# Windowed differential attention: all rotated tiles, spreads and v ahead of the loop, the shifted v by a transfer inside SBUF, the normalisation in three pieces

## The chip, the cores and the metric

One Trainium2 chip, one core. The metric is the time of one execution on the device in microseconds, the median over several runs. The kernel is one program for the whole network below.

## What is computed

The input x is 1024 tokens by 256 features. Eight sublayers follow each other, each x = layernorm(x + f(x)): causal attention, an 8-bit gated MLP, windowed differential attention, a mixture of experts, causal attention, a binary-weight linear layer, attention with a multiplied mask, a ternary gated MLP. The change is in the third. Cut to what matters:

```python
q = (x @ Wq).reshape(b, s, 16, 16).transpose(0, 2, 1, 3)     # 16 heads of 16
k = (x @ Wk).reshape(b, s, 4, 16).transpose(0, 2, 1, 3)      # 4 key/value heads
v = (x @ Wv).reshape(b, s, 4, 16).transpose(0, 2, 1, 3)
q = q * cos + rotate_half(q) * sin;  k = k * cos + rotate_half(k) * sin
k, v = repeat(k, 4), repeat(v, 4)
a1 = q[..., :8] @ k[..., :8].T * 8 ** -0.5
a2 = q[..., 8:] @ k[..., 8:].T * 8 ** -0.5
allowed = (col <= row) & (col >= row - 63)
p1, p2 = softmax(a1 + neg), softmax(a2 + neg)
diff = relu(p1 - lam * p2)
diff = diff / (diff.sum(-1) + 1e-6)
out = (diff @ v) @ Wo
x = layernorm(x + out)
```

## The kernel before

Each engine has its own program, written out by hand, and they meet on semaphores. TensorE (PE), VectorE (DVE), ScalarE (ACT) and GpSimd (POOL) compute; SP issues the transfers. PE writes into two double banks of PSUM called pair (a ring: a new use waits until ACT has read the one before the last), three banks called bank (a ring read by DVE) and pvb.

**Tiles.** The tokens are in two halves of 512; the second half comes first, here and in the neighbouring sublayers. A tile of q or k is 128 (q) or 64 (k) rows of features by 512 tokens, so there are three a half: k, q of heads 0 to 7, q of heads 8 to 15. `W_HALVES` lists the six, and ("R", i) stands for the i-th. For each, PE makes two products with the plain and the swapped weights (`tile_rows`, L1654, matmuls at L1481), DVE multiplies them by cos and sin and adds them (`rotate`, L1228 and L1231), ACT rounds to bf16 (`highest`, L915), DVE takes the remainder and rounds it (`middle`, L1239 and L1240), and POOL takes the last remainder (`lowest`, L781). The three bf16 parts sit in `piece`; w_buf, where the rotation is written, has two buffers, and rotation i waits for the low part of i - 2.

**Spreads.** An item ("s", side, g, x, half) lays two heads' parts out over the partitions, with six selector matmuls on PE (L1673) into one pair, and ACT copies the pair to SBUF as bf16 (L930 ahead of the loop, L937 in it). Twenty are needed in all: for each half, two of k and eight of q. Six of them precede the loop today.

**The order.** `windowed_plan` returns two lists. All engines walk through both, each doing its share of every item. `W_BEFORE` is the opening; today R0 (whose half is ready early), then x1 (transposes of the other half of x, L1486, and ACT's copies to xT, L827), R1, R2, and six spreads. `W_PLAN` is the loop over 32 units. A unit k is a tile t of 128 queries by a group g of four heads, in the order of `T_ORDER`: token tiles 5, 6, 7, 4, then 0 to 3. In step k:

- ("S", k): PE writes the mask and the scores of both softmaxes into a pair (L1722, L1728); DVE takes the maxima (L1268); ACT takes eight exponentials with their sums (L948); in the next step DVE makes the ratio of the sums (L1251, L1252) and POOL forms lam * p2 - p1 (L797, L800).
- ("uT", k - 3): PE transposes that (L1752), DVE applies the relu and stores it (L1286).
- every fourth step pv: PE multiplies by v (L1768), ACT copies pvb (L954), and a step later accT: PE transposes back (L1775), DVE divides (L1296 to L1298).
- after the 16 units of the first half: outT (L1486 bank<-A, L1302), four projections with residual and statistics (L1049, L1053), then ("norm"), all of `normalise(s, 0)` in one step: 4 aggregations, 3 small steps and 3 times 3 Newton steps (L1065 to L1075), 4 products (L1077).

Into these steps today's plan puts the rest of the preparation: spreads of q groups 2 and 3 in steps 0 and 1, R3, R4, R5 in steps 2, 4, 6, v in step 3, the ten spreads of the other half in steps 6 to 15 (one each). Spreads in the loop share the ring of pairs with the scores.

**v.** The window of a 64-query block reaches 64 tokens back, so v is needed twice: `v_own` with the tokens of a tile on its 128 partitions, and `v_back`, the same shifted by 64 tokens. Both are projected: PE makes two sets of eight small products in two banks (L1736 to L1745), and DVE copies them (L1281, L1283, L1284).

After the loop `last_half_out` transposes, projects and normalises the other half; the mixture of experts follows.

On SP, in this sublayer, two loads of weights are issued when the sublayer before is normalised (`load(WF...)`, `load(WA[0]...)`); what follows in SP's queue waits for xn_ready of this sublayer.

## Time and profile before

| | us |
|---|---|
| median of 3 runs (lowest, highest) | 1172.81 (1171.85, 1173.26) |
| profiled execution, its own time | 1171.49 |
| its span, first to last instruction | 1169.7 |
| PE busy | 1005.7 (86%) |
| DVE busy | 698.5 (60%) |
| ACT busy | 541.8 (46%) |
| POOL busy | 332.7 (28%) |
| mean granted clock of PE | 0.907 |

The times in all rows count from the span's start. A row of the timeline gives start, duration, engine, line, operation, output<-input, the shapes and a count where equal instructions are merged, then in brackets how long the engine had been idle and who released it. The granted clock of PE is 1.00 (2.4 GHz) or 0.50 (1.2 GHz) at any moment; a figure between is a mean. The changed stage runs from 266.5 (its first tile) to 460.

### The profile page before, as it was taken

What the parts mean: (1) busy time and instruction counts of PE and PEld (TensorE: products, weight loads), DVE (VectorE), ACT (ScalarE), POOL (GpSimd) and SP (SyncE); (2) the same over time, 40 slices, a digit from 0 to 9 for tenths busy, and PEclk for the clock granted to TensorE, in tenths of its full rate; (3) what the DMA queues carried; (4) which work ended last, traced back from release to release, by engine and by line L of the source; (5) the groups of instructions that cost most, each with busy time, mean ns of one, the idle gap of its engine ahead of it and who ended that gap; (6) DMA issues with size and microseconds to landing.
All of it is one profiled execution on the core that took longest, in us unless ns stands there. A gap on an engine that the chain in (4) does not pass through costs nothing. (4 is left out here: it accounts for less than half of the span.)

```text
span 1169.7 us, 16510 instructions
## 1 busy us (share of the span) xinstructions
PE 1005.7 (86%) x5954; PEld 573.3 (49%) x5954; DVE 698.5 (60%) x1986; ACT 541.8 (46%) x1145; POOL 332.7 (28%) x464
## 2 busy tenths in 40 slices
PE   6999998787998868899998899887777988888785
PEld 2545454673444535337356444444454544445575
DVE  2667773775376873532322358778282677876665
ACT  3566655333579862110112456664314455556422
POOL 3202122331367870000002111112461144532222
PEclk9989998998789977899998969999778889999898
DMA  5000000103000002000000002000000000000000
GB/s 229 1 1 1 1 1 1 50 1 159 1 1 2 2 1 92 14 1 1 0 1 1 0 1 109 1 1 1 1 1 1 0 1 1 2 1 1 1 18 19
DMA packets 4165, 21.12 MB, mean 18 GB/s; under 512 B 345, under 2 KB 1625, under 8 KB 3060
## 3 DMA queue, kind: packets, MB, share of 16 engines
q1 hardware_dynamic: 4084, 20.06, 4.4%
q8 instruction: 48, 0.79, 0.3%
q14 instruction: 33, 0.27, 0.1%
HBM read 19.01 MB, written 1.05 MB: 17 GB/s over the span
## 5 line engine op out<-in xcount | busy, mean ns | idle before, releaser
L890 ACT ACTIVATE PB<-pair 128x1024 f32<-128x1024 f32 (+3 forms) x288 | 223.1, 811 | 140.8 <-PE pair L1609 139.6
L1126 DVE CUSTOM_DVE_ANT_0 junk<-bank,cst 128x128 bf16<-128x128 f32 (+3 forms) x384 | 171.5, 487 | 127.8 <-PE bank L1593 125.7
L724 POOL TENSOR_SCALAR_AFFINE_SELECT PB<-PB 128x256 f32<-128x256 f32 x192 | 79.0, 415 | 330.4 <-ACT PB L890 328.7
L1129 DVE TENSOR_REDUCE pmx<-bank 128x1 f32<-128x512 f32 x192 | 122.8, 684 | 49.7 <-PE bank L1593 48.9
L1593 PE MATMUL bank<-KO_r,QO_r 64*128 64x512 f32 (+3 forms) x576 | 138.4, 417 | 11.7 <-DVE A L1204 3.9
L1625 PE MATMUL pvb<-PB,V 128*32 128x512 f32 (+3 forms) x1152 | 128.2, 517 | 11.8 <-ACT PB L890 8.2
L1605 PE MATMUL pair<-QO_r,KO_r 64*128 64x512 f32 (+3 forms) x576 | 115.7, 393 | 15.8 <-ACT PB L890 14.8
L1593 PEld LDWEIGHTS bank<-KO_r,QO_r 64*128 64x128 f32 x576 | 71.6, 191 | 111.7 <-DVE pmx L1126 40.2
L730 POOL TENSOR_TENSOR parts_r<-y_f,parts_r 128x512 fp32r<-128x512 f32 x24 | 30.6, 1276 | 321.2 <-ACT parts_r L861 321.2
L1609 PE MATMUL pair<-ms,sel_r 64*128 64x512 f32 (+3 forms) x576 | 102.5, 349 | 0.0
L948 ACT ACTIVATE KO<-pair,nm 128x128 f32<-128x128 f32 x256 | 91.6, 434 | 22.1 <-DVE nm L1268 22.0
L1605 PEld LDWEIGHTS pair<-QO_r,KO_r 64*128 64x128 f32 x576 | 56.5, 190 | 69.0 <-ACT PB L890 55.6
L1049 DVE TENSOR_TENSOR X<-bank,X 128x256 f32<-128x256 f32 x56 | 23.7, 424 | 86.0 <-PE bank L1870 43.9
L970 ACT ACTIVATE PB<-pair 128x512 f32<-128x512 f32 (+1 forms) x28 | 16.7, 597 | 125.5 <-PE pair L1481 125.5
L1481 PE MATMUL pair<-xT,WA 128*128 128x512 f32 x96 | 59.3, 759 | 10.4 <-DMA WA<-in_w_att 8.0
L797 POOL TENSOR_SCALAR KO<-KO,cc,cst 128x128 f32<-128x128 f32 x128 | 55.9, 454 | 38.6 <-DVE cc L1252 38.1
L948 ACT ACTIVATION_READ_ACCUMULATOR KO<-pair,nm 128x1 f32 x256 | 65.1, 273 | 0.0
L1609 PEld LDWEIGHTS pair<-ms,sel_r 64*128 64x128 f32 x576 | 57.7, 191 | 4.1
L1268 DVE TENSOR_REDUCE nm<-pair 128x4 f32<-128x512 f32 x64 | 42.4, 685 | 24.9 <-PE pair L1728 24.4
L1481 PE MATMUL pair<-xT,WF 128*128 128x512 f32 (+1 forms) x112 | 57.1, 633 | 0.0
L1412 DVE TENSOR_TENSOR PB<-bank,PB 128x512 f32<-128x512 f32 (+1 forms) x28 | 19.4, 691 | 60.5 <-PE bank L1481 60.4
L1481 PE MATMUL bank<-xT,WF 128*128 128x512 f32 (+1 forms) x112 | 54.5, 610 | 0.0
(208 smaller groups left out, 1686.5 us busy)
## 6 DMA issues: line engine op xcount, KB each, us to landing
WF<-in_moe_gu SPq DMA_DIRECT2D x1, 3520.0 KB, 10.8
WA<-in_w_att SPq DMA_DIRECT2D x3, 1024.0 KB, 10.3
WF<-in_tern_w SPq DMA_DIRECT2D x1, 3072.0 KB, 11.1
V<-in_moe_d SPq DMA_DIRECT2D x1, 1792.0 KB, 7.2
xT<-in_xT SPq DMA_DIRECT2D x2, 512.0 KB, 5.9
X<-in_x SPq DMA_DIRECT2D x1, 1024.0 KB, 10.9
A<-in_rope SPq DMA_DIRECT2D x1, 1024.0 KB, 4.7
out<-X SPq DMA_DIRECT2D x2, 512.0 KB, 2.9
```

Source lines behind the costliest of these rows:

```text
L724: pool.affine_select(p2, p2, pattern=[[0, 2], [1, P]], compare_op=ALU.is_ge, fill=0.0, base=0, channel_multiplier=-1).then_inc(causal, 1)
L797: last = pool.tensor_scalar(e2[:, hh, :], e2[:, hh, :], cc[:, k % 4, 1, hh:hh + 1], lam, ALU.mult, ALU.mult)
L890: act.activation(pb[:, st % 2, 2 * i:2 * i + 2, 0:n], ps[:, :, 0:n], ACT.Exp, scale=scale)\
L948: last = act.activation(ew[k % EW][:, z, hh, :], slot[:, z, hh * P:(hh + 1) * P], ACT.Exp, bias=nm2[:, (2 * k + z) % 4, hh:hh + 1], accum_ ...
L1126: r_done(dve.tensor_tensor_reduce(junk[:, (r_used - 1) % 3, 0:n], ps[:, 0:n], tri[:, HALF - n:HALF], 1.0, LOWEST, ALU.add, ALU.max, accum_ ...
L1129: r_done(dve.tensor_reduce(to, ps[:, 0:n], AX.X, ALU.max))
L1268: dve.tensor_reduce(nm2[:, (2 * k + z) % 4, :], pair[(n // 2 - 1) % 2][:, z, :].rearrange("p (h n) -> p h n", h=HG), AX.X, ALU.max, negate ...
L1481: last = pe.matmul(ps, w(c), x(c), start=(c == 0), stop=(c == ND - 1))
L1593: pe.matmul(r_slot()[:, 0:n], qd[rows, TWO * g + i, t * P:(t + 1) * P], kd[rows, TWO * g + i, c * HALF:c * HALF + n], start=True, stop=Tru ...
L1605: pe.matmul(ps[:, j, 0:n], kd[rows, TWO * g + i, kb * P:(kb + 1) * P], qd[rows, TWO * g + i, q0:q0 + n], start=True, stop=False)
L1609: last = pe.matmul(ps[:, j, 0:n], sel_r[rows, 2 * TWO + i, :], ms[rows, b, q0 - qh * HALF:q0 - qh * HALF + n], start=False, stop=True)
L1625: last = pe.matmul(pvb[j * STRIP:(j + 1) * STRIP, q0 - qh * HALF:HALF], v_all[:, kb, g * HG + j, :], pb[:, st % 2, j, 0:n], start=(kb == 0 ...
```

## The change

All six tiles are rotated in `W_BEFORE`, in the order k, k of the other half, q, q of the half that is used first, q, q of the other; so are twelve of the twenty spreads and v. The other eight spreads (q of the other half) come in steps 1, 3, ... 15. `T_ORDER` becomes 4, 5, 6, 7, 0 to 3. On each engine the item's share stands where the item stands, and each of DVE's `middle(i - 1)` follows `rotate(i)`. v is projected once, and v_back is filled by two transfers on SP, from partitions 0 to 63 of v_own to 64 to 127 and the reverse, one tile on; PE waits for them before the first pv. The normalisation of the first half is spread over three steps. The split_x that is removed stood under a condition that doesn't hold for this sublayer. The diff, without its empty lines and the two new semaphores:

```diff
--- before.py
+++ after.py
@@ -131,7 +131,8 @@
 E_EXP = NG * 12 * 2
-E_USES = {ATT: 8 + 4 * NG + TH + E_EXP + 2 * NG + 8, WATT: 12, GLU: 2 * NF + 4, MOE: 2 * NF_MOE + 4, BIN: 4, TERN: 2 * NF + 4}
+W_E = ND + 12 + 2 * ND
+E_USES = {ATT: 8 + 4 * NG + TH + E_EXP + 2 * NG + 8, WATT: W_E, GLU: 2 * NF + 4, MOE: 2 * NF_MOE + 4, BIN: 4, TERN: 2 * NF + 4}
@@ -385,36 +386,28 @@
-W_TILES = (2, 0, 1)
-W_HALVES = [(tile, half) for half in halves_in(SUBLAYERS.index(WATT)) for tile in W_TILES]
-W_LAST, W_FIRST = TH * halves_in(SUBLAYERS.index(WATT))[1], TH * halves_in(SUBLAYERS.index(WATT))[0]
-T_ORDER = [W_FIRST + k for k in (1, 2, 3, 0)] + [W_LAST + k for k in range(TH)]
+W_SOON, W_LATE = halves_in(SUBLAYERS.index(WATT))
+W_OUT, W_END = halves_out(SUBLAYERS.index(WATT))
+W_FIRST = TH * W_OUT
+W_HALVES = [(2, W_SOON), (2, W_LATE)] + [(tile, half) for half in (W_OUT, W_END) for tile in range(2)]
+T_ORDER = [TH * half + k for half in (W_OUT, W_END) for k in range(TH)]
 UNITS = [(t, g) for t in T_ORDER for g in range(NG)]
-    first, second = W_HALVES[0][1], W_HALVES[-1][1]
-    def rows(side, g, half):
-        return [("s", side, g, x, half) for x in range(TWO)]
-    before = [("R", 0), ("x1",), ("R", 1), ("R", 2)] + rows("k", 0, first) + rows("q", 0, first) + rows("q", 1, first)
-    after = {k: [] for k in range(len(UNITS))}
-    after[0] = rows("q", 2, first)
-    after[1] = rows("q", 3, first)
-    for i, k in ((3, 2), (4, 4), (5, 6)):
-        after[k].append(("R", i))
-    after[3].append(("v",))
-    for x in range(TWO):
-        after[6 + x].append(("s", "k", 0, x, second))
-        for g in range(NG):
-            after[8 + TWO * g + x].append(("s", "q", g, x, second))
+    def rows(side, groups, half):
+        return [("s", side, g, x, half) for g in groups for x in range(TWO)]
+    before = [("R", 0), ("x1",), ("R", 1), ("R", 2), ("R", 3)] + rows("k", (0,), W_SOON) + rows("k", (0,), W_LATE) \
+        + rows("q", (0, 1), W_OUT) + [("R", 4)] + rows("q", (2, 3), W_OUT) + [("R", 5), ("v",)]
+    late = rows("q", range(NG), W_END)
     plan = []
             plan.append(("S", k))
-            plan += after[k]
+            if k % 2 and late:
+                plan.append(late.pop(0))
         else:
@@ -425,8 +418,9 @@
         step = j - NG * TH - 2
-        if 0 <= step < 6:
-            plan.append([("outT",), ("proj", 0), ("proj", 1), ("proj", 2), ("proj", 3), ("norm",)][step])
+        if 0 <= step < 8:
+            plan.append([("outT",), ("proj", 0), ("proj", 1), ("proj", 2), ("proj", 3), ("norm", 0), ("norm", 1),
+                         ("norm", 2)][step])
     last = NT - 1
@@ -470,7 +464,7 @@
     for item in W_BEFORE + W_PLAN:
-        n += {"R": 2, "v": 2, "uT": 1, "accT": 1, "outT": ND, "proj": 1}.get(item[0], 0)
+        n += {"R": 2, "v": 1, "uT": 1, "accT": 1, "outT": ND, "proj": 1}.get(item[0], 0)
         if item == ("uT", gi):
@@ -680,6 +675,12 @@
                     load(WA[0][:, :], t_in["w_att2"], ld_att2)
+                    sp.wait_ge(v_there, 1)
+                    sp.wait_ge(w_blank, 1)
+                    v_from, v_to = (v.rearrange("p t h c -> p (t h c)") for v in (v_own, v_back))
+                    row = KV * STRIP
+                    load(v_to[WIN:P, :], v_from[0:WIN, :], v_moved)
+                    load(v_to[0:WIN, row:], v_from[WIN:P, 0:(NT - 1) * row], v_moved)
             for k, half in enumerate(halves_out(len(SUBLAYERS) - 1)):
@@ -781,11 +782,9 @@
-            for i in range(3):
+            for i in range(len(W_HALVES)):
                 lowest(i)
             for item in W_PLAN:
-                if item[0] == "R":
-                    lowest(item[1])
                 if item[0] in ("S", "flush") and 1 <= item[1] <= len(UNITS):
@@ -929,8 +928,6 @@
                 for item in W_PLAN:
-                    if item[0] == "R":
-                        highest(item[1])
                     if item[0] == "s":
@@ -1059,24 +1056,30 @@
-            def normalise(s, k):
+            def normalise(s, k, which=(0, 1, 2)):
                 t0 = halves_out(s)[k] * TH
-                for t in range(t0, t0 + TH):
-                    last = dve.bn_aggr(mv[:, t, :], stats[:, t, :])
-                step(last)
                 v, y, w = lnv[:, 0, :], lnv[:, 1, :], lnv[:, 2, :]
-                step(dve.tensor_scalar(v, mv[:, t0:t0 + TH, 1], EPS, None, ALU.add))
-                step(dve.tensor_scalar(y.bitcast(I32), v.bitcast(I32), 1, None, ALU.logical_shift_right))
-                step(dve.tensor_scalar(y.bitcast(I32), y.bitcast(I32), -1.0, float(0x5F3759DF), ALU.mult, ALU.add))
-                for _ in range(3):
+                def refine():
                     step(dve.scalar_tensor_tensor(w, y, -0.5, y, ALU.mult, ALU.mult))
                     step(dve.scalar_tensor_tensor(y, w, 1.5, y, ALU.add, ALU.mult))
-                for t in range(t0, t0 + TH):
-                    dve.tensor_scalar(X[:, t, :], X[:, t, :], mv[:, t, 0:1], lnv[:, 1, t - t0:t - t0 + 1],
-                                      ALU.subtract, ALU.mult).then_inc(xn_ready, 1)
-                dve.wait_ge(xn_ready, NT * s + TH * (k + 1))
+                if 0 in which:
+                    for t in range(t0, t0 + TH):
+                        last = dve.bn_aggr(mv[:, t, :], stats[:, t, :])
+                    step(last)
+                    step(dve.tensor_scalar(v, mv[:, t0:t0 + TH, 1], EPS, None, ALU.add))
+                    step(dve.tensor_scalar(y.bitcast(I32), v.bitcast(I32), 1, None, ALU.logical_shift_right))
+                    step(dve.tensor_scalar(y.bitcast(I32), y.bitcast(I32), -1.0, float(0x5F3759DF), ALU.mult, ALU.add))
+                if 1 in which:
+                    for _ in range(3):
+                        refine()
+                if 2 in which:
+                    for t in range(t0, t0 + TH):
+                        dve.tensor_scalar(X[:, t, :], X[:, t, :], mv[:, t, 0:1], lnv[:, 1, t - t0:t - t0 + 1],
+                                          ALU.subtract, ALU.mult).then_inc(xn_ready, 1)
+                    dve.wait_ge(xn_ready, NT * s + TH * (k + 1))
@@ -1257,8 +1260,13 @@
                             middle(i - 1)
-                middle(2)
-                turned = []
+                    if item[0] == "v":
+                        middle(len(W_HALVES) - 1)
+                        ps = r_slot()[:, :].rearrange("p (t h d) -> p t h d", t=NT, h=KV)
+                        last = dve.tensor_copy(v_own[:, :, :, 0:HD], ps)
+                        r_done(last)
+                        r_wait()
+                        dve.nop().then_inc(v_there, 1)
                 for item in W_PLAN:
@@ -1268,20 +1276,8 @@
                                               AX.X, ALU.max, negate=True).then_inc(wmax_ready, 1)
-                        if turned:
-                            middle(turned.pop())
                     if item[0] in ("S", "flush") and 1 <= item[1] <= len(UNITS):
                         ratio(item[1] - 1)
-                    if item[0] == "R":
-                        rotate(item[1])
-                        turned.append(item[1])
-                    if item[0] == "v":
-                        dve.wait_ge(w_blank, 1)
-                        ps = r_slot()
-                        r_done(dve.tensor_copy(v_own[:, :, :, 0:HD], ps[:, :].rearrange("p (t h d) -> p t h d", t=NT, h=KV)))
-                        ps = r_slot()[:, :].rearrange("p (t h d) -> p t h d", t=NT, h=KV)
-                        step(dve.tensor_copy(v_back[WIN:P, 0, :, 0:HD], ps[WIN:P, 0, :, :]))
-                        r_done(dve.tensor_copy(v_back[:, 1:NT, :, 0:HD], ps[:, 1:NT, :, :]))
                     if item[0] == "uT":
@@ -1303,9 +1299,7 @@
                     if item[0] == "norm":
-                        normalise(s, 0)
-                if SUBLAYERS[s + 1] in (GLU, TERN):
-                    split_x(s + 1, 0)
+                        normalise(s, 0, item[1:])
                 post(s, 1)
@@ -1686,14 +1680,19 @@
                         last.then_inc(e_full, 1)
+                    if item[0] == "v":
+                        w = w_att(s, 2 * D + 2 * KV * HD, KV * HD)
+                        ps = r_slot()
+                        for t in range(NT):
+                            last = over_width(ps[:, t * KV * HD:(t + 1) * KV * HD], lambda c: xT[:, c, t * P:(t + 1) * P],
+                                              lambda c: w[:, c, :])
+                        last.then_inc(r_full, 1)
                 uT_at = {}
                 for item in W_PLAN:
-                    if item[0] == "R":
-                        tile_rows(item[1])
                     if item[0] == "s":
@@ -1705,15 +1704,9 @@
                         n = w_banks(item)
-                        if k in (2, 3):
-                            pe.wait_ge(w_free, w_banks(("s", "q", g, 1, W_HALVES[0][1])))
-                        if t == W_FIRST or k == NT // 2 * NG:
-                            pe.wait_ge(w_free, w_banks(("s", "k", 0, 1, W_HALVES[-1][1])))
-                        if k >= NT // 2 * NG and t == W_LAST:
-                            pe.wait_ge(w_free, w_banks(("s", "q", g, 1, W_HALVES[-1][1])))
+                        if ("s", "q", g, TWO - 1, t // TH) in W_RING:
+                            pe.wait_ge(w_free, w_banks(("s", "q", g, TWO - 1, t // TH)))
                         for z in range(2):
@@ -1729,21 +1722,6 @@
                             last.then_inc(w_full, 1)
-                    if item[0] == "v":
-                        w = w_att(s, 2 * D + 2 * KV * HD, KV * HD)
-                        x_ready(halves_in(s)[1])
-                        ps = r_slot()
-                        for t in range(NT):
-                            last = over_width(ps[:, t * KV * HD:(t + 1) * KV * HD], lambda c: xT[:, c, t * P:(t + 1) * P],
-                                              lambda c: w[:, c, :])
-                        last.then_inc(r_full, 1)
-                        ps = r_slot()
-                        over_width(ps[WIN:P, 0:KV * HD], lambda c: xT[:, c, 0:WIN], lambda c: w[:, c, :])
-                        for t in range(1, NT):
-                            last = over_width(ps[:, t * KV * HD:(t + 1) * KV * HD],
-                                              lambda c: xT[:, c, t * P - WIN:t * P + WIN], lambda c: w[:, c, :])
-                        last.then_inc(r_full, 1)
-                        v_at = r_used
                     if item[0] == "uT":
@@ -1757,7 +1735,8 @@
                         if n == 0:
-                            pe.wait_ge(r_free, v_at)
+                            pe.wait_ge(v_there, 1)
+                            pe.wait_ge(v_moved, 32)
```

## Rows read from the trace of the kernel before

**Rows 1.** Stretches of the stage: us, then busy us of PE, PEld, DVE, ACT, POOL.

```profile
272.24:294.08 21.84, 16.69 (x76) 6.80 (x78) 10.77 (x16) 10.06 (x12) 4.34 (x5) 0.81 0.53 213
294.08:375.10 81.02, 72.30 (x578) 35.63 (x573) 47.34 (x100) 61.72 (x276) 48.53 (x78) 0.84 0.01 1
375.10:432.40 57.30, 45.51 (x439) 26.98 (x437) 49.13 (x120) 47.70 (x261) 46.66 (x79) 0.82 0.01 2
432.40:448.40 16.00, 9.22 (x53) 6.16 (x52) 5.23 (x12) 3.42 (x7) 4.79 (x8) 0.71 0.00 0
```

**Rows 2.** Timeline, ACT: start us, us, what [idle before, releaser].

```profile
294.08 0.37 ACT L948 ACTIVATE KO<-pair,nm 128x128 f32<-128x128 f32 x1 [0.76 <-DVE nm L1268]
...
322.71 0.37 ACT L948 ACTIVATE KO<-pair,nm 128x128 f32<-128x128 f32 x1 [5.73 <-DVE nm L1268]
...
352.07 0.42 ACT L948 ACTIVATE KO<-pair,nm 128x128 f32<-128x128 f32 x1
...
355.72 0.48 ACT L948 ACTIVATE KO<-pair,nm 128x128 f32<-128x128 f32 x1
...
416.76 0.37 ACT L948 ACTIVATE KO<-pair,nm 128x128 f32<-128x128 f32 x1 [5.06 <-DVE nm L1268]
```

**Rows 3.** Timeline, the opening: PE's transposes and tiles, ACT's xT.

```profile
272.25 1.09 PE L1486 MATMUL pair<-cst,X 128*128 128x128 f32 x8 [2.14 <-DVE X L1077]
...
273.18 7.03 PE L1481 MATMUL bank<-xT,WA 128*128 128x512 f32 x16
...
274.79 1.06 ACT L827 ACTIVATE xT<-pair 128x512 f32<-128x512 f32 x2
```

**Rows 4.** The same opening, a tile's chain (the L1240 row: ns min/median/max).

```profile
272.23 1.28 DVE L1228 SCALAR_TENSOR_TENSOR rest<-bank,A 64x512 f32<-64x512 f32 x2
...
277.54 0.69 DVE L1231 TENSOR_TENSOR y_f<-y_f 128x512 f32<-128x512 f32 x1
...
278.26 0.63 ACT L915 ACTIVATE parts<-y_f 128x512 bf16<-128x512 f32 x1 [2.42 <-DVE y_f L1231]
...
279.48 1.15 POOL L781 TENSOR_TENSOR parts<-rest,parts 64x512 bf16<-64x512 f32 x1 [6.66 <-DVE parts L1240]
...
285.62 5.34 PE L1673 MATMUL pair<-parts,junk 32*128 32x512 bf16 x24 [3.37 <-POOL parts L781]
...
290.99 1.02 ACT L930 ACTIVATE QO<-pair 128x1024 bf16<-128x1024 f32 x1 [0.26 <-PE pair L1673]
...
L1240 DVE CAST parts<-rest x3: 418/427/1259, 279.0 to 329.9; 128x512 bf16<-128x512 f32 x2, 64x512 bf16<-64x512 f32 x1
```

**Rows 5.** Busy time and granted clock of three stretches: us, PE, PEld, DVE, ACT, POOL, PEclk.

```profile
285.00:290.00 5.00, 4.38 (x22) 1.48 (x24) 0.76 (x1) 2.50 (x4) 1.62 (x2) 0.57 0.00 0
350.00:375.00 25.00, 20.60 (x223) 9.90 (x224) 15.28 (x36) 25.00 (x113) 20.00 (x34) 1.00 0.01 2
425.00:430.00 5.00, 5.00 (x43) 2.64 (x43) 3.53 (x8) 4.53 (x25) 4.64 (x10) 0.50 0.02 3
```

**Rows 6.** Timeline, PE in the loop: a spread; tile R3.

```profile
294.35 1.46 PE L1673 MATMUL pair<-parts,junk 32*128 32x512 bf16 x6
...
306.93 4.94 PE L1481 MATMUL bank<-xT,WA 128*64 128x512 f32 x8
```

**Rows 7.** Timeline, the v projection on PE and the first copy on DVE.

```profile
313.13 7.43 PE L1481 MATMUL bank<-WA,xT 128*128 128x64 f32 x64
...
317.02 0.69 DVE L1281 COPY V<-bank 128x512 f32<-128x512 f32 x1 [1.06 <-PE bank L1481]
```

**Rows 8.** The normalisation on DVE: first row, last row; all L1074 (ns min/median/max).

```profile
410.38 0.36 DVE L1065 BATCH_NORM_AGGREGATE mv<-stats 128x2 f32<-128x6 f32 x4
...
414.56 1.38 DVE L1077 TENSOR_SCALAR X<-X,mv,lnv 128x256 f32<-128x256 f32 x4
...
L1074 DVE TENSOR_TENSOR lnv<-lnv x48: 161/162/1119, 175.7 to 1164.6; 128x4 f32<-128x4 f32 x48
```

**Rows 9.** The page's DMA issues: KB each, us from issue to landing.

```profile
V<-in_moe_d SPq DMA_DIRECT2D x1, 1792.0 KB, 7.2
```

More of the change, by code:

```diff
@@ L623, in build @@
         w_blank = sem("w_blank")
+        v_there, v_moved = sem("v_there"), sem("v_moved")
         ratio_ready = sem("ratio_ready")
```

## The prediction

> **What bounds the kernel now.** The change touches one sublayer, the windowed differential attention, so I read that stage, in four views. First the busy time by stretch [rows 1]. The stage is an opening of 21.84 us, from the last input tile to the first exponential; then 32 units (a tile of 128 queries by a group of four heads), of which the first 16 take 81.02 us and the last 16 57.30 us; then a tail of 16.00 us. In the first 16 ACT is busy for 61.72 us of 81.02, in the last 16 for 47.70 of 57.30. No engine is full in any of them: what counts is which engine is waited for at each hand-over.
>
> Second, ACT's own timeline [rows 2]. Where ACT is kept fed, one unit and one spread copy take 355.72 - 352.07 = 3.65 us, and that is 2.74 us of exponentials (eight at 0.343) and 0.9 for the copy. Where it is not, it waits for DVE's maxima L1268: 5.73 us at 322.71, behind the v projection, and 5.06 us at 416.76, behind the normalisation. So ACT sets the pace when nothing is in its way, and the loss of the first half, 81.0 against about 60, comes from rotations and projections that sit in the loop.
>
> Third, the opening [rows 3, 4]: a chain that goes from PE to DVE to ACT and POOL and back for every tile, with PE mostly waiting. Fourth, the granted clock [rows 5]: 1.00 until 285, where PE had been idle for 3.37 us, then 0.50 (1.2 GHz); it comes back during tile R3, which starts at 306.93, and is at 0.50 again behind the normalisation.
>
> **The opening, step by step.** The change takes all six rotated tiles, twelve spreads and the v projection ahead of the loop. Nothing of the loop runs beside them, so every wait in the chain counts.
> 1. The second tile is now the key tile of the other half, whose xT ACT writes at 274.79 to 275.85 [rows 3]. PE starts it at 275.9, where today it starts a query tile at 273.18. PE has then done only 1.09 us of transposes since 270.1. I expect half the clock for its first part: 4.94 us as at 306.93 [rows 6], not 7.03/2 = 3.5. It ends at 280.8.
> 2. From there the chain goes by rows 3 and 4. Last product 0.2 after PE, then 0.69, sum 0.69: 282.5. Middle part: a subtraction like the sum, 0.69, and a cast of 0.42, with gaps: 283.7. Low part on POOL 1.15: 284.9. Next rotation, 1.28 + 0.69 with gaps: 286.9. Middle 288.1, low 289.3, next rotation 291.4, ACT's high part 0.63: 292.0. ACT's queue has four such high parts ahead of its first spread copy, so that copy starts at 292.05.
> 3. Eight copies. Two spreads are ready, a copy is 1.02 [rows 4] (292.05, 293.1); PE has by then idled over 3.37 us, so the third takes 1.46 us at half clock (294.6), and the other five follow by today's spacing of 1.30 (PE's 24 matmuls in 5.34 us, one copy to each six) [rows 4]: the last spread ends at 301.1.
> 4. The fifth tile, 4.94: 306.05. DVE's last product and sum 307.7, middle of the fourth tile 308.9, low part 310.1. The fourth tile's spreads wait for that, because its middle part stands behind the fifth rotation on DVE. Four spreads, 1.46 + 3 x 1.30: 315.5. Sixth tile, 4.94: 320.4. Rotation 322.0, middle 323.2, middle of the sixth 324.4.
> 5. That last one runs beside POOL's low part; one cast in that place took 1.26 instead of 0.43 [rows 4], so 325.2. The v copy of 0.69: 325.9. v itself takes PE about 3.85 us (today 313.13 to the copy at 317.02 [rows 7]), ends at 324.3 and is hidden. First maximum 0.69, first exponential 326.8. Today it is at 294.08 [rows 2]. **Opening: +32.7 us.**
>
> **The first 16 units.** ACT's busy 61.72 loses six spread copies (14 to 8, about 1.0 each) and three high parts (1.9): 53.8. Stalls: PE idles after the first two units, until the first pair of banks is free, and works at half clock. There PE needs 3.0 us a unit without a spread (it is full while ACT, whose units are 2.74, is busy 4.53 of 5 us: 2.74 x 5/4.53 [rows 5]) and 0.7 for half a spread of 1.46 [rows 6], so 3.7 against ACT's 2.74 + 0.45 = 3.2 or a little less with pauses. I take three units at 0.7 with what queues behind a spread, 2.0 in all, before PE, now without pause, has its clock back. Together 55.8 against 81.02: **-25.2 us.** At full clock nothing holds ACT: from 350 to 375 today, with a spread in each unit where there will be one in two, it is busy 25.00 us of 25, and PE 20.60 [rows 5].
>
> **The last 16 units.** The normalisation holds DVE from 410.38 to 415.94, the cost of ACT's 5.06 [rows 8, 2]. Its three pieces are 1.0 (0.36 and three small steps of 0.2, 0.16 and a gap), 1.8 (nine such steps) and 1.5 us (1.38 and a wait), each behind a unit's maxima, ratio and transposed copy. DVE is busy 49.13 of 57.30 [rows 1], 0.5 us free a unit, so ACT waits about 0.4, 1.0 and, where accT (about 1.0) comes in the same step, 2.1: saved 1.5. Behind the hole today's last four units run at clock 0.50 with ACT busy 4.53 of 5.00 [rows 5]: 0.3 a unit, 1.1 in all. **-2.6 us.** The stalls at outT and at the projections stay: nothing there is changed.
>
> **What costs nothing.** The second v product goes (PE about 3.6, half of 7.43 [rows 7], and two copies on DVE): it is inside the 25.2. The two transfers that take its place wait on SP for the v copy; the queue behind them holds only loads that wait for this sublayer's last tile anyway. No transfer inside SBUF stands in the trace. The nearest row is 7.2 us for 1792 KB in [rows 9]; these are 256 KB each, so I take 0 to 7.2 us, and up to the first pv in step 7 there are at least seven units of 2.74, 19 us. The order of the second half's tiles (4, 5, 6, 7 for 5, 6, 7, 4) is of equal work; "second half first" is so today. The split_x that goes never ran here. The tail: 0, perhaps -1 if it starts at the full clock.
>
> **Sum:** 32.7 - 25.2 - 2.6 = +4.9 us. The profiled run took 1171.49 (span 1169.7), so 1176.4 there; the median is 1.32 above it, so 1177.7. What a measurement of this kernel can tell from no change is 0.2%, or 2.3 us.
>
> **Rivals.** *The opening keeps the full clock* (the other side). Its tiles are dense work, and the idle stretches before R1 (2.6 us) and between tiles are near one that today did not lower the clock (2.14 us before 272.25 [rows 3]). Then R1 and the two late tiles save 1.45 each (4.3), the spreads follow ACT's 1.02 and not 1.30 (2.2), the third and ninth save 0.65 each (1.3), the loop's first stalls 2.0: 9.8 us less, 1168. It decides at the half: from about 7 us of these the kernel is faster. Against it: steps 3 and 4 leave PE idle for over 3.4 us by the chain alone, as much as before 285.62. *The loop gains more*: with no tiles in it, DVE has slack, all three norm pieces hide (3.5) and the tail gains 1: 1173.2, no change. *The loop stays slow*: PE with pauses does not win its clock back, as from 286 to 307 today. With pv and its transpose (some 0.4) PE needs 4.1 us a unit at half clock, 0.9 more than ACT; five units more of that than booked: +4.6, 1182.3.
>
> A row speaks on the norm pieces too: one of the nine small steps took 1.12 us, not 0.16, while POOL's subtraction ran [rows 8]; the others, some of them beside POOL as well, were not stretched, and I book nothing. The Trainium skill says more (GPSIMD Engine Reference, Specifications): GpSimd shares its SBUF interfaces with VectorE, and DVE instructions with two SBUF inputs contend. By that rule each piece, met by one POOL subtraction a unit, would wait about 1 us once: some 2 us more and 1179.7, inside the slow case. The trace agrees in part.
>
> **Chances.** Forecast (+2.5 to +7) 0.50, loop stays slow 0.16, no net change 0.17, opening at full clock 0.17. So faster 0.17, same 0.17, slower 0.66. Range: 1168 (the full-clock case) to 1183 (the slow loop).
>
> **What would show it.** First exponential 32.7 us after today's (step by step: R1 starting 2.7 late and taking 4.9; first spread copy at 292; the fourth tile's low part holding the ninth spread); unit 17 7.5 us late; the last exponential 4.9 late; ACT's wait behind the norm in three parts that sum to 3.5. Wrong if the clock stays 1.00 in the opening, if pv waits for the transfers, or if ACT waits in the first 16 units more than 4 us in all.

## The result, and the profile after

| | us |
|---|---|
| before, median of 4 runs (lowest, highest) | 1172.33 (1171.37, 1173.26) |
| after, median of 4 runs (lowest, highest) | 1189.66 (1189.29, 1190.34) |
| ratio of the times, 95% interval | 1.0134, 1.0100 to 1.0168 |
| span of the profiled execution, before and after | 1169.7, 1188.2 |
| mean granted clock of PE, before and after | 0.907, 0.885 |

The change makes the kernel slower by 17.3 us where +4.9 was forecast: the sign is right, the size lies above the range. Executions of the kernel before lay between 1169.71 us at a mean granted clock of 0.906 and 1179.77 us at 0.894, so every kernel below is compared by its ratio to before from the same group of runs.

First the busy time by stretch of the kernel after, in the four stretches of [rows 1] (opening, first 16 units, last 16 units, the start of the tail), and a fifth inside the first 16 units. The columns are the window, its length, PE, PEld, DVE, ACT and POOL busy with their counts, the granted clock, the DMA share and GB/s.

```profile
274.08:328.39 54.31, 44.18 (x188) 18.24 (x188) 20.85 (x33) 18.08 (x21) 7.80 (x8) 0.78 0.21 86
328.39:392.10 63.71, 56.59 (x429) 26.52 (x426) 37.81 (x81) 54.62 (x268) 44.96 (x75) 0.62 0.04 9
392.10:451.00 58.90, 47.92 (x446) 28.28 (x442) 50.38 (x121) 47.21 (x260) 46.07 (x78) 0.82 0.01 1
451.00:468.00 17.00, 10.73 (x51) 6.96 (x51) 4.28 (x12) 3.87 (x7) 4.93 (x8) 0.53 0.00 1
330.70:358.00 27.30, 26.11 (x175) 11.67 (x177) 14.62 (x31) 24.70 (x121) 20.97 (x35) 0.51 0.01 2
```

Against the same stage of before, measured from the same transposes of x1 (272.25 there [rows 3]), the opening grew by 32.5 us (forecast 32.7), the first 16 units shrank by 17.4 (forecast 25.2), and the last 16 grew by 1.7 (forecast: shrink by 2.6); unit 17 starts at 375.15 there, and a stretch of units ends with the last exponential. So the opening is as forecast, and what was missed is in the loop, 7.8 and 4.3 us. ACT's busy 54.62 us in the first 16 units is near the 53.8 of the working; the other 9.09 us of the 63.71 are waits, where 2.0 were booked. The last row says what is special: for 27 us PE is busy 26.11 of 27.30, and its clock is 0.51. Before, a stretch of the same loop with more matmuls in each unit ran at 1.00 with PE busy 20.60 of 25 [rows 5]. The high busy share goes with the half clock: the same six spread matmuls take 1.46 us at it and 0.82 at the full one.

The clock did come back in the first half, at 357.7, 374.7 and 391.7, but the first two times only for some 7 us. PE then waited for ACT three times (0.88, 0.30 and 0.66 us before 362.04, 363.74 and 365.14), and from 365.14 on its matmuls took the times of the half clock again. Two stretches of the kernel after, columns as above:

```profile
358.00:365.00 7.00, 5.30 (x62) 2.93 (x58) 6.20 (x15) 5.72 (x33) 4.62 (x9) 0.97 0.00 1
365.00:374.70 9.70, 9.56 (x67) 4.38 (x67) 4.29 (x10) 8.09 (x36) 7.37 (x12) 0.50 0.01 2
```

All three units with a pv step fell into stretches at the half clock.

The opening on PE, the timeline of the kernel after, answers [rows 3, 4, 6]; a row gives start, duration, engine, line, operation and, in brackets, the idle time and the releaser.

```profile
277.73 13.12 PE L1475 MATMUL bank<-xT,WA 128*64 128x512 f32 x24 [2.56 <-ACT xT L826]
...
295.80 7.61 PE L1667 MATMUL pair<-parts,junk 32*128 32x512 bf16 x36 [3.54 <-ACT KO L929]
303.34 5.25 PE L1475 MATMUL bank<-xT,WA 128*128 128x512 f32 x8
312.61 4.72 PE L1667 MATMUL pair<-parts,junk 32*128 32x512 bf16 x24 [4.02 <-POOL parts L782]
317.27 5.12 PE L1475 MATMUL bank<-xT,WA 128*128 128x512 f32 x8
```

Three tiles run through without a gap, then PE waits 3.54 us for ACT and 4.02 us for the fourth tile's low part, and each single tile behind such a wait takes 5.1 to 5.3 us, not the 3.5 of the full clock.

A unit with a pv step in the slow loop, on PE, and what ACT does about it (the releaser L1276 is DVE's maxima, as in [rows 2]):

```profile
369.38 1.46 PE L1667 MATMUL pair<-parts,junk 32*128 32x512 bf16 x6
370.77 1.94 PE L1747 MATMUL pvb<-PB,V 128*32 128x256 f32 x16
372.64 1.12 PE L1730 MATMUL bank<-cst,KO 128*128 128x128 f32 x4
373.55 0.63 PE L1715 MATMUL pair<-wmaskb,idb 128*128 128x512 bf16 x1
```

```profile
372.83 0.64 ACT L951 ACTIVATE acc<-pvb 128x512 f32<-128x512 f32 x1
...
375.57 0.37 ACT L945 ACTIVATE KO<-pair,nm 128x128 f32<-128x128 f32 x1 [2.10 <-DVE nm L1276]
```

Spread, pv and transposes stand ahead of the next scores on PE and take 4.2 us at the half clock, more than ACT's one unit of 2.74. The same three before the change, on PE's timeline of the kernel before:

```profile
355.99 0.82 PE L1673 MATMUL pair<-parts,junk 32*128 32x512 bf16 x6 [0.18 <-ACT QO L937]
356.74 1.07 PE L1768 MATMUL pvb<-PB,V 128*32 128x256 f32 x16
357.75 0.66 PE L1752 MATMUL bank<-cst,KO 128*128 128x128 f32 x4
358.24 0.38 PE L1722 MATMUL pair<-wmaskb,idb 128*128 128x512 bf16 x1
```

They take 2.25 us, and ACT doesn't wait. After, the three units with a pv step in the first half take 6.1 to 6.4 us each and hold 6.0 of the 9.09 us of waits (1.80, 2.10, 2.10).

In the last 16 units ACT waits behind the three pieces of the norm, ACT's timeline of the kernel after:

```profile
431.36 0.37 ACT L945 ACTIVATE KO<-pair,nm 128x128 f32<-128x128 f32 x1 [0.91 <-DVE nm L1276]
...
436.86 0.37 ACT L945 ACTIVATE KO<-pair,nm 128x128 f32<-128x128 f32 x1 [2.11 <-DVE nm L1276]
...
442.52 0.37 ACT L945 ACTIVATE KO<-pair,nm 128x128 f32<-128x128 f32 x1 [2.76 <-DVE nm L1276]
```

The transfers answer [rows 9]. The page's rows of DMA issues give KB each and us from issue to landing:

```profile
V<-V SPq DMA_DIRECT2D x1, 256.0 KB, 3.1
V<-V SPq DMA_DIRECT2D x1, 224.0 KB, 3.5
```

The two were issued from 327.61 on, and PE's first pv stands at 354.58: nobody waits for them.

### The profile page after: what moved, and what is told of

It is laid out like the page before. It is cut to its first block and busy times, and to the rows that moved or that the text cites. A ratio compares the mean times of both kernels' runs of the same rounds, so it can differ in the third digit from the quotient of the medians.

```text
span 1188.2 us, 16450 instructions
## 1 busy us (share of the span) xinstructions
PE 1021.2 (86%) x5922; PEld 576.7 (49%) x5922; DVE 700.4 (59%) x1984; ACT 542.0 (46%) x1145; POOL 331.7 (28%) x464
## 3 DMA queue, kind: packets, MB, share of 16 engines
HBM read 19.01 MB, written 1.05 MB: 17 GB/s over the span
## 5 line engine op out<-in xcount | busy, mean ns | idle before, releaser
L945 ACT ACTIVATION_READ_ACCUMULATOR KO<-pair,nm 128x1 f32 x256 | 61.9, 243 | 0.0
L1276 DVE TENSOR_REDUCE nm<-pair 128x4 f32<-128x512 f32 x64 | 42.4, 687 | 12.9 <-PE pair L1721 12.4
```

The costliest lines, as they stand in the source:

```text
L945: last = act.activation(ew[k % EW][:, z, hh, :], slot[:, z, hh * P:(hh + 1) * P], ACT.Exp, bias=nm2[:, (2 * k + z) % 4, hh:hh + 1], accum_ ...
L1276: dve.tensor_reduce(nm2[:, (2 * k + z) % 4, :], pair[(n // 2 - 1) % 2][:, z, :].rearrange("p (h n) -> p h n", h=HG), AX.X, ALU.max, negate ...
```

## The experiments

Eleven kernels were run. The kernel before was timed beside each group of runs, and its median moved from 1172.55 to 1177.73 between groups, which is why ratios are compared, not times. The stage tables read one profiled execution each; lengths that depend on the clock differ by some us from one execution to the next, so a column counts only where the ratios say the same.

**Which part of the change costs the time.** Four kernels take the parts one by one. `b_norm3` is the kernel before with the three norm pieces:

```diff
-        if 0 <= step < 6:
-            plan.append([("outT",), ("proj", 0), ("proj", 1), ("proj", 2), ("proj", 3), ("norm",)][step])
+        if 0 <= step < 8:
+            plan.append([("outT",), ("proj", 0), ("proj", 1), ("proj", 2), ("proj", 3), ("norm", 0), ("norm", 1),
+                         ("norm", 2)][step])
```

> Kernel before with only the normalisation in three pieces. Theory A (the three pieces bring nothing, because two-input DVE steps beside POOL's subtraction are stretched and accT stands in the same step): within 2 us of before; ACT's waits at units 27 to 29 sum to 4.5 to 6 us, as against 5.06 in one. Theory B (recorded forecast: the pieces save 1.5 us of wait and keep the clock up): 1170, waits of 3.5 us.

Measured: 1172.65 us, ratio 1.0002 (0.9976 to 1.0028). No gain and no loss. ACT's waits behind the three pieces are 0.91, 1.50 and 2.76 us, 5.2 in sum, against 5.06 in one.

`b_vdma` is the kernel before with v projected once, in step 3 where it was, and the two transfers:

```diff
+                    load(v_to[WIN:P, :], v_from[0:WIN, :], v_moved)
+                    load(v_to[0:WIN, row:], v_from[WIN:P, 0:(NT - 1) * row], v_moved)
...
-                        step(dve.tensor_copy(v_back[WIN:P, 0, :, 0:HD], ps[WIN:P, 0, :, :]))
-                        r_done(dve.tensor_copy(v_back[:, 1:NT, :, 0:HD], ps[:, 1:NT, :, :]))
...
-                        over_width(ps[WIN:P, 0:KV * HD], lambda c: xT[:, c, 0:WIN], lambda c: w[:, c, :])
```

> Kernel before with only the shifted v by two transfers, v still in step 3 of the loop. PE loses 3.6 us of small products that stand before unit 4's scores. Theory A (the first half is bound by the queue on PE): 3 to 4 us faster, 1169, the wait of 5.73 us at unit 4 shrinks to about 2. Theory B (pv waits for the transfers, which cost the change its time): no faster or slower than before, with PE waiting at the first pv.

Measured: 1171.5 us, ratio 0.9986 (0.9970 to 1.0002), where 3 to 4 us less were expected; the interval takes in no change. ACT's wait behind v falls from 5.73 us [rows 2] to 2.15, in ACT's timeline of this kernel:

```profile
318.77 0.37 ACT L955 ACTIVATE KO<-pair,nm 128x128 f32<-128x128 f32 x1 [2.15 <-DVE nm L1275]
```

So these 3.6 us were saved, and in the profiled execution they were lost again. The clock fell between 360 and 368, and ACT waited 0.59, 2.10 and 0.45 us at 367.95, 374.35 and 377.69, where it waits nothing before, and 5.4 us at outT and the projections against 3.8. The stretch of `b_vdma`, then ACT behind its pv step:

```profile
368.00:376.00 8.00, 8.00 (x68) 3.73 (x62) 3.82 (x9) 5.90 (x28) 3.38 (x6) 0.62 0.01 3
```

```profile
374.35 0.37 ACT L955 ACTIVATE KO<-pair,nm 128x128 f32<-128x128 f32 x1 [2.10 <-DVE nm L1275]
```

The wait behind a pv step at the half clock is therefore not peculiar to the kernel after. The plan of before has it too when its clock falls, 2.10 us also in `b_both` (at 373.88) and `b_norm3` (at 381.27).

`b_both` has both, with tiles, spreads and v still in the loop:

> Kernel before with both small parts, all tiles still in the loop. Theory A (the loss of the change is the preparation moved ahead): 1168 to 1171, so the move alone costs 18 to 21 us. Theory B (the loss comes from the small parts): 1180 or more.

Measured: 1171.45 us, ratio 0.9980 (0.9964 to 0.9995). And `a_norm1` is the kernel after with the norm in one step:

```diff
-        if 0 <= step < 8:
-            plan.append([("outT",), ("proj", 0), ("proj", 1), ("proj", 2), ("proj", 3), ("norm", 0), ("norm", 1),
-                         ("norm", 2)][step])
+        if 0 <= step < 6:
+            plan.append([("outT",), ("proj", 0), ("proj", 1), ("proj", 2), ("proj", 3), ("norm", 0, 1, 2)][step])
```

> Changed kernel with the normalisation in one step again. Theory A (pieces bring nothing): within 2 us of the changed kernel, 1188 to 1191. Theory B (they save what I forecast): 2 to 4 us slower, 1192 to 1194.

Measured: 1189.58 us, ratio 1.0137 (1.0113 to 1.0162), the same as the kernel after. So the two small parts give 0.2%, and the move of the preparation, with the order of tiles that goes with it, takes all of the loss: from 0.998 to 1.0134, 18 us.

**Whether the clock is the cause.** PE's programs get idle matmuls, work that nobody reads, in stretches where PE would wait; no part of the computation is left out.

```diff
+                def fill(n):
+                    for _ in range(n):
+                        pe.matmul(pvb[:, :].rearrange("p (h n) -> p h n", h=HG), idb[:, :],
+                                  wmaskb[:, 0:1, :].to_broadcast([P, HG, P]), start=True, stop=True)
...
+                pe.wait_ge(acc_ready, ACC0[s])
+                pe.wait_ge(cast_ready, 2)
...
+                    if item == ("R", 1):
+                        fill(12)
+                    if item == ("s", "k", 0, 0, W_LATE):
+                        fill(14)
+                    if item[0] == "s" and W_BEFORE[n - 1] == ("R", 4):
+                        fill(16)
```

`a_warm_open` is the kernel after with these three. `a_warm` has them and more in the loop:

```diff
+                    if item[0] == "s" and W_PLAN[n - 1] == ("S", 1):
+                        fill(12)
+                    if item[0] == "S" and W_PLAN[n - 1][0] in ("uT", "accT") and (item[1] < 8 or item[1] % NG):
+                        fill(2)
```

> Changed kernel with idle matmuls (into a free bank, nobody reads them) in three gaps of the opening: 12 before the second tile, 14 before the third spread, 16 before the ninth. Theory C (the opening is long by its chain of hand-overs; the clock adds some 7 us): clock near 1.00 through the opening, first exponential 5 to 8 us earlier than in the changed kernel, time 1182 to 1185. Theory D (the clock in the opening costs little): within 2 us of the changed kernel.

> As a_warm_open, with idle matmuls in the loop too: 12 before the first spread, 2 before a unit's scores in three steps of four. Theory C (the first 16 units take 63.7 us instead of the 55.8 forecast because PE, with one spread for two units, pauses too often and its clock falls): clock over 0.95 from unit 4 on, first 16 units in 55 to 58 us, time 1172 to 1178. Theory D (the pv step itself stalls the loop, whatever the clock): the 2.1 us waits at units 8, 12, 16 stay and the added matmuls make it slower, 1184 to 1190.

Measured: `a_warm_open` 1183.67 us, ratio 1.0070 (1.0043 to 1.0097), and `a_warm` 1175.41 us, ratio 1.0000 (0.9979 to 1.0022). The busy time by stretch of `a_warm`, opening, first 16 and last 16 units, then two stretches of its first 16 units:

```profile
272.55:322.91 50.36, 48.26 (x224) 21.09 (x224) 20.84 (x33) 17.76 (x22) 7.80 (x8) 0.90 0.23 93
322.91:380.87 57.96, 51.00 (x470) 25.06 (x470) 39.36 (x82) 53.80 (x268) 44.30 (x75) 0.88 0.04 10
380.87:436.69 55.82, 45.31 (x454) 26.42 (x452) 50.58 (x121) 47.31 (x261) 46.83 (x79) 0.94 0.01 2
337.50:347.00 9.50, 9.50 (x65) 4.61 (x60) 4.82 (x11) 6.80 (x34) 5.99 (x10) 0.56 0.01 2
347.00:380.87 33.87, 29.59 (x323) 15.29 (x321) 26.84 (x57) 33.87 (x169) 29.32 (x50) 1.00 0.01 2
```

The opening is 3.95 us shorter, the first 16 units 5.75, the last 16 units 3.1, with more matmuls on PE. In `a_warm_open` the opening is the same 50.35 us and the first 16 units are 64.03: a fast opening does not help the loop. The opening's clock is 0.90 with the idle matmuls, above the 0.81 before [rows 1], and it is still 28.5 us longer than before: that much is the chain of hand-overs and not the clock. In the loop of `a_warm` the clock came later than expected: in units 5 to 7 ACT still waits 1.46, 1.15 and 1.55 us, at a clock of 0.56, and from 347 on it is 1.00 and ACT is busy 33.87 of 33.87 us. A unit with a pv step takes 4.13 us there instead of 6.4, and ACT no longer waits in it; PE's timeline of `a_warm`:

```profile
363.44 0.82 PE L1667 MATMUL pair<-parts,junk 32*128 32x512 bf16 x6 [0.74 <-ACT KO L945]
364.19 1.07 PE L1764 MATMUL pvb<-PB,V 128*32 128x256 f32 x16
365.20 0.66 PE L1747 MATMUL bank<-cst,KO 128*128 128x128 f32 x4
365.69 0.38 PE L1732 MATMUL pair<-wmaskb,idb 128*128 128x512 bf16 x1
```

**Whether real work does it too.** `a_dense` is the kernel after with one late spread in each of steps 0 to 7, one to a unit as in steps 6 to 15 of before, in place of one in two:

```diff
-            if k % 2 and late:
+            if late:
```

> Changed kernel with the eight late spreads in steps 0 to 7, one each, so the same work earlier. Theory C (pauses of PE lower the clock): denser PE work in units 1 to 8, full clock there sooner, but lighter units 9 to 16 with less; in all within 3 us of the changed kernel, with the half-clock stretches moved behind unit 8. Theory D (the count of spreads beside a unit sets its time, not the clock): units 1 to 8 slower by 4 x 0.9, units 9 to 16 faster by the same, no net change and the 2.1 us waits where they are.

Measured: 1185.86 us, ratio 1.0100 (1.0063 to 1.0137). The first 16 units take 60.25 us and the last 57.11; ACT waits 0.8, 0.8, 0.7, 0.7, 2.1 and 1.1 us ahead of units 5 to 10, and behind them no more in the first half. That is about 4 us less than the kernel after by the ratios, but their intervals overlap, so a gain is not shown. Denser work did not bring the clock back sooner either: it is 0.50 from 345 to 360 with PE busy all the time, and comes back at 368. And it then stays at 1.00 through units that have no spread at all:

```profile
370.00:388.69 18.69, 13.94 (x176) 7.89 (x172) 16.10 (x37) 18.62 (x106) 17.58 (x30) 1.00 0.01 3
```

PE is busy 13.94 of 18.69 us there, with single waits of 1.43 and 1.27 us, a share no larger than the 5.30 of 7.00 behind which the kernel after lost its clock. So the runs show what the half clock costs this loop, but not what makes it fall: thin work alone does not explain it.

**Whether the opening's order matters.** `a_order` keeps tiles and spreads ahead of the loop in the order k, q, q of one half, then the other:

```diff
-W_HALVES = [(2, W_SOON), (2, W_LATE)] + [(tile, half) for half in (W_OUT, W_END) for tile in range(2)]
+W_HALVES = [(tile, half) for half in (W_SOON, W_LATE) for tile in (2, 0, 1)]
...
-    before = [("R", 0), ("x1",), ("R", 1), ("R", 2), ("R", 3)] + rows("k", (0,), W_SOON) + rows("k", (0,), W_LATE) \
-        + rows("q", (0, 1), W_OUT) + [("R", 4)] + rows("q", (2, 3), W_OUT) + [("R", 5), ("v",)]
+    before = [("R", 0), ("x1",), ("R", 1), ("R", 2)] + rows("k", (0,), W_SOON) + rows("q", (0, 1), W_OUT) \
+        + [("R", 3)] + rows("q", (2, 3), W_OUT) + [("R", 4)] + rows("k", (0,), W_LATE) + [("R", 5), ("v",)]
```

> Changed kernel with the tiles of the first half rotated first in the opening (k, q, q, then k, q, q of the other half), spreads placed as soon as their tile allows. Theory C (the second tile waits for xT, and four high parts stand ahead of the first spread copy): first tile pair without the 2.6 us gap and the half clock in it, first copy some 8 us earlier, but four hand-overs of tile and spread after it instead of three; first exponential 2 to 6 us earlier, 1183 to 1188. Theory D (any order of the serial chain costs the same): within 2 us.

Measured: 1189.29 us, ratio 1.0124 (1.0087 to 1.0160), with an opening of 55.86 us. This order makes the opening no shorter.

**What is left when both have the clock.** `b_warm` is `b_both` with idle matmuls (`fill` as above):

```diff
+                    if item == ("s", "q", 0, 0, W_HALVES[0][1]):
+                        fill(14)
...
+                    if n in (2, 5):
+                        fill(4)
+                    if n in (3, 6):
+                        fill(3)
+                    if item[0] == "S" and W_PLAN[n - 1][0] in ("uT", "accT") and (item[1] < 8 or item[1] % NG):
+                        fill(2)
```

> The kernel before with shifted v by transfers and the norm in pieces (the run that came out at 0.998 of before), the tiles still in the loop, plus idle matmuls in TensorE's gaps: 14 ahead of the first q spread of the opening, 4 and 3 around the extra spreads of steps 0 and 1, 2 ahead of the scores behind each uT or accT. Theory (the clock that TensorE keeps through its gaps sets the time of its spread and pv matmuls): the granted clock of the span rises from about 0.90 to at least 0.92, the opening falls from 21.9 to about 19 to 21 us, units 1 to 16 from 79.2 to 75 to 78 us, the whole to 1163 to 1170 us, ratio 0.992 to 0.997. Rival (ACT's exponentials set the loop of the kernel before, TensorE has time to spare at either clock): the opening and the loop stay within 1 us, ratio 0.998 to 1.002. Second rival (idle matmuls are work in the way): units 1 to 16 grow by over 1 us and the ratio is above 1.002.

Measured: 1167.4 us, ratio 0.9929 (0.9901 to 0.9957), faster than both kernels. Its three stretches:

```profile
271.57:292.94 21.37, 18.74 (x92) 7.84 (x94) 10.78 (x16) 9.95 (x13) 4.35 (x5) 0.89 0.54 219
292.94:369.32 76.38, 72.35 (x580) 33.29 (x575) 47.63 (x98) 61.65 (x276) 48.72 (x78) 0.90 0.03 8
369.32:425.87 56.55, 46.54 (x454) 27.03 (x452) 51.12 (x121) 47.37 (x261) 46.52 (x79) 0.90 0.01 2
```

Against `a_warm`, with like clocks, the opening is 29.0 us shorter and the first 16 units 18.4 us longer. So of the 18 us that the move costs, some 8 (1.0000 against 0.9929) stay when both have idle matmuls, placed differently in each: the chain ahead of the loop costs more than its work costs inside it. The first two units take 8.1 us each where before they took 6.3: there the idle matmuls stand in the way. Whether fewer of them would be better wasn't tried.

**Why the norm pieces gain nothing.** In the kernel after, DVE's three pieces and what POOL does beside them:

```profile
429.13 0.36 DVE L1070 BATCH_NORM_AGGREGATE mv<-stats 128x2 f32<-128x6 f32 x4
...
433.44 0.22 DVE L1066 SCALAR_TENSOR_TENSOR lnv<-lnv 128x4 f32<-128x4 f32 x1
...
434.32 1.13 DVE L1066 SCALAR_TENSOR_TENSOR lnv<-lnv 128x4 f32<-128x4 f32 x1
...
439.12 2.58 DVE L1080 TENSOR_SCALAR X<-X,mv,lnv 128x256 f32<-128x256 f32 x4
```

```profile
434.16 1.27 POOL L799 TENSOR_TENSOR KO<-KO 128x512 f32<-128x512 f32 x1
...
439.64 1.26 POOL L799 TENSOR_TENSOR KO<-KO 128x512 f32<-128x512 f32 x1
```

The small step that starts within POOL's subtraction ends with it (434.32 + 1.13 against 434.16 + 1.27), and the four products take 2.58 us where they took 1.38 [rows 8]. `b_warm_sep` moves each piece on DVE to directly behind the maxima, ahead of the ratio that starts POOL's work; `b_warm_one` is `b_warm` with the norm in one step. The edit of `b_warm_sep` against `b_warm`:

```diff
+NORM_IN = {NG * TH + 5 + 5 + w: (w,) for w in range(3)}
...
+                        if k in NORM_IN:
+                            normalise(s, 0, NORM_IN[k])
                     if item[0] in ("S", "flush") and 1 <= item[1] <= len(UNITS):
                         ratio(item[1] - 1)
...
-                    if item[0] == "norm":
-                        normalise(s, 0, item[1:])
```

> As the kernel before with v by transfers, three norm pieces and idle matmuls (the run that came out at 0.993 of before), but on DVE each norm piece stands directly behind the maxima of its step, ahead of the ratio that sets POOL to work, and not at the end of the step. The instructions are the same; only what POOL does beside them changes. Theory (the pieces are stretched because POOL works beside them): the four products of the third piece take 1.4 us instead of 2.6, the nine small steps 1.6 to 1.9 instead of about 3, ACT's three waits behind the norm sum to 3.5 us or less instead of 5.8, and the kernel is 1.5 to 2.5 us faster than with the pieces at the end of the step. Rival (the pieces cost what DVE has no free time for, wherever they stand): the durations shrink but the waits stay at 5 us or more. Second rival: the stretching does not come from POOL, and the durations stay.

> The same kernel with idle matmuls and v by transfers, with the whole norm in one step as in the kernel before. Theory (pieces and one step cost the same, as in the pair without idle matmuls, 5.8 us of ACT's waits against 5.1): within 1.5 us of the run with three pieces, one wait of 5.0 to 5.6 us behind the norm. Rival (three holes are better than one long one, which lowers the clock for the units behind it): 1.5 to 3 us slower than with the pieces.

Measured: `b_warm_sep` 1164.67 us, ratio 0.9921 (0.9892 to 0.9949), and `b_warm_one` 1165.45 us, ratio 0.9922 (0.9893 to 0.9951): all three placements are one within the measurement. In the traces ACT's waits behind the norm are 0.28, 1.74 and 2.53 us (4.6 in sum) in `b_warm_sep`, 5.8 in `b_warm`, and one of 5.08 in `b_warm_one`, which has two more of 1.05 and 0.78 in the units behind it. The theory for `b_warm_sep` failed: the four products took 2.35 us and not 1.4, the waits sum to more than 3.5, and the kernel is not measurably faster than `b_warm`. Its premise was not met, since POOL was not out of the way. It was a unit behind, so its subtraction still met the pieces, DVE and POOL of `b_warm_sep`:

```profile
405.64 1.13 DVE L1078 SCALAR_TENSOR_TENSOR lnv<-lnv 128x4 f32<-128x4 f32 x1
...
410.33 2.35 DVE L1092 TENSOR_SCALAR X<-X,mv,lnv 128x256 f32<-128x256 f32 x4
```

```profile
405.48 1.26 POOL L809 TENSOR_TENSOR KO<-KO 128x512 f32<-128x512 f32 x1
...
410.62 1.26 POOL L809 TENSOR_TENSOR KO<-KO 128x512 f32<-128x512 f32 x1
```

The instructions with POOL idle beside them are there in the kernel before, whose norm in one step held up POOL too; POOL's timeline of the kernel before:

```profile
411.85 1.27 POOL L800 TENSOR_TENSOR KO<-KO 128x512 f32<-128x512 f32 x1
417.71 1.74 POOL L797 TENSOR_SCALAR KO<-KO,cc,cst 128x128 f32<-128x128 f32 x4 [4.59 <-DVE cc L1252]
```

From 413.12 to 417.71 POOL has nothing to do, and there, from 414.56 on, the four products take 1.38 us [rows 8]. In pieces, each meets a POOL at work. One exception is in `b_warm_sep`: two small steps of the first piece ran while POOL was idle, from 402.69 on. They took 0.17 us each, where the kernel after has 0.38 and 0.39, and ACT's wait was 0.28 us against 0.94 in `b_warm`. The durations follow POOL in all these traces; that they alone keep ACT waiting is not shown, since no run had the other two pieces beside an idle POOL.

## Why the prediction was right or wrong, point by point

- **The opening, +32.7 us: right, 32.5.** Step 1: the second tile starts 3.65 us after the transposes, as worked out, with half the clock for its first part. Step 2: the first spread copy comes 20.6 us after them, forecast 19.8. Steps 3 and 4: the ninth spread waits for the fourth tile's low part, at 38.5 (forecast 37.9), and the sixth tile stands at 43.2 (forecast 43.3); the late tiles take 5.1 to 5.3 us, forecast 4.94. Step 5: the last cast took the 1.26 us that was foreseen. The first exponential comes after 54.3, forecast 54.55. The rival with the full clock in the opening priced that clock at 7.8 us in the opening itself; `a_warm_open`, whose clock there is 0.90, gives 4.0.
- **The first 16 units, -25.2: wrong, -17.4.** The step that failed is "three units at 0.7 with what queues behind a spread, 2.0 in all, before PE, now without pause, has its clock back". PE was busy without pause for 27 us and did not have its clock back: 0.51 from 330.7 to 358.0. Later it had it for some 7 us at a time and lost it again, 0.62 over the stretch. The stalls are 9.09 us, not 2.0, and the sign that was named for this, over 4 us of ACT's waits, came. The third rival, that the loop stays slow, names this mechanism, but priced it at 0.9 for five units; it left out that spread, pv and transposes in one unit queue up to 4.2 us ahead of the scores, and those three units alone are 6.0 us. `a_warm` shows it by bringing the clock back: 57.96 us, and these three waits gone. Why the clock fell again in the kernel after is not shown.
- **"At full clock nothing holds ACT": right,** in `a_warm` from its eighth unit on ACT has no wait in the first half. But the row that I took for it, 350 to 375 with 1.00 [rows 5], was from a loop with other work in each unit, and the rate read there holds only at its clock. The kernel after did not keep that clock. The expectation of `a_warm` put this down to PE's thinner work; `a_dense`, which kept the clock in units without any spread, speaks against that as the whole reason.
- **The last 16 units, -2.6: wrong, +1.7.** The three pieces' waits are 0.91, 2.11 and 2.76, 5.8 in sum, against 0.4, 1.0 and 2.1, 3.5: 2.3 too little. The step that failed is "the others were not stretched, and I book nothing": on DVE the pieces took 1.4, 3.0 and 2.6 us, not 1.0, 1.8 and 1.5. The first was mis-sized for another reason, since its steps already took 1.45 us before (410.38 to 411.83), two of them 0.39 and 0.40 and not 0.16. The units behind the hole did run without waits, but that was 0.7 us, not 1.1. And "the stalls at outT and at the projections stay" is off by 1.6: they sum to 5.4 us against 3.8 before, with PE's clock at 0.52 from 409 to 416; `b_vdma` shows the same 2.0 us wait there, and in `a_warm` they are 3.2. It goes with the clock and not with the tiles.
- **The rule on the shared interfaces** (the Trainium skill, GPSIMD Engine Reference, Specifications: VectorE instructions with two SBUF inputs contend with GpSimd) had "some 2 us more" by my working. The waits came out 2.3 us longer, so the size fits. The trace agrees with the rule for the small steps: one with two SBUF inputs took 1.13 us beside POOL's subtraction, and the reciprocal L1254, with one input, 0.17 beside another (427.97). The four products have one large SBUF input and were stretched too, 2.58 for 1.38, which the rule as I used it does not say. I weighed it by the eight unstretched small steps, and seven of them ran while POOL stood idle (from 413.12 on).
- **What costs nothing: right.** The transfers took 3.1 and 3.5 us inside the bound of 7.2, and PE never waited for them. That the second v product is gone is worth 0.14% alone (`b_vdma`), and its interval takes in nothing at all. The tail: +0.5 (13.27 against 12.73 us to the next copies).
- **Not in the sum:** the transposes of x1 came 1.8 us later than before in this execution (274.08 against 272.25), in a part that the change doesn't touch; in the other kernels they lie between 271.6 and 273.9 with either plan. The profiled spans differ by 18.5 us: 32.5 - 17.4 + 1.7 + 0.5 + 1.8 = 19.1, and the rest, -0.6, lies behind the stage.

## What to carry to other kernels

A rate read in a stretch belongs to that stretch's clock. When a change alters PE's work in a loop (preparation hoisted out of it, spreads one in two), ask at which clock the changed loop will run, and price each unit's PE queue at the half clock too, the unit with the most in front of its scores first. Where that price is far from the other, the range has to hold both. Preparation that looks like a loss inside a loop may be what is cheapest there: hoisted, its chain PE-DVE-ACT-POOL ran alone, and 32 us of it bought 17. And cutting a long step into pieces gained nothing here: DVE had 0.5 us free a unit, the waits were 4.6 to 5.8 us in three pieces and 5.1 in one, and no time told them apart.

## What the runs showed of the hardware that was not expected

- PE was busy 26.11 of 27.30 us at a granted clock of 0.51; a high busy share is therefore no sign of the full clock. Before, PE was busy 20.60 of 25 us at 1.00, and in `a_dense` 13.94 of 18.69 us at 1.00.
- Idle matmuls that add work to PE made a kernel faster: by 1.3% from the kernel after to `a_warm` and by 0.5% from `b_both` to `b_warm`.
- A copy inside SBUF of 256 KB on half the partitions took 3.1 us from issue to landing.
- A VectorE instruction with two inputs of 128x4 elements, all in SBUF, that takes 0.16 us alone took up to 1.13 us beside POOL's subtraction, and ended with it, while a reciprocal on 128x4, with one input, took 0.17 beside it (at 427.97), and the maxima L1276, which read PSUM, took 1.29 us for two with a subtraction beside them (at 423.76 in the kernel after) and with POOL idle (at 441.73).
